# Shared-expert weights loaded at the head of the last attention body, its products spread over three chunks, the fourth part placed behind the body

## What is computed

```
x = x + tanh(g_xattn) * attention(layernorm(x), ctx_1024, ctxb_2048x32)
# attention: softmax(Q K^T * gate / sqrt(32)) V, then @ Wo + bo
xn = layernorm(x)
gs, us = xn @ wg_s, xn @ wu_s
out = (silu(gs) * us) @ wd_s                 # shared expert
out = out + sum over the top 2 of 16 experts of weight * ((silu(g) * u) @ wd_r)
x = x + tanh(g_ffn) * out
```

## Time and profile before

| what | value |
|---|---|
| median of 3 runs | 2016.85 us (2014.12 to 2017.68) |
| profiled execution, its own time | 2012.53 us |
| its span | 2010.8 us |
| PE busy | 1920.7 us (96%) |
| DVE / ACT / POOL busy | 1110.7 / 784.5 / 1225.4 us |
| DMA | 331.82 MB, mean 165 GB/s |
| last attention body | about 1376.4 to 1463.8 us |
| what stands behind it, up to the experts' phase | 1463.8 to 1499.1 us |

### The profile page before, as it was taken

One profiled execution on the slowest core, in us unless ns is written; L12 is line 12 of the kernel. 1 busy time (PEld: TensorE's weight loads), 2 busy tenths in 40 slices (PEclk: granted clock), 3 DMA queues, 4 the chain that ended last, 5 costly groups with the idle time before them and its releaser, 6 DMA issues. The chain is left out here.

```text
span 2010.8 us, 40479 instructions
## 1 busy us (share of the span) xinstructions
PE 1920.7 (96%) x12469; PEld 1494.6 (74%) x12470; DVE 1110.7 (55%) x1765; ACT 784.5 (39%) x1557; POOL 1225.4 (61%) x1383
## 2 busy tenths in 40 slices
PE   6799999999999999999999999999879999999799
PEld 5587877878787787878778787786658766666587
DVE  4556565656556566565656656565447533333287
ACT  3244454444545444454444445454432122222000
POOL 2377677776867777677777767675522533332463
PEclk9899999999999999999999999999889999999899
DMA  6754848466483755738375483746135454444787
GB/s 220 199 142 126 228 108 221 120 172 179 127 240 97 197 149 144 209 114 234 104 188 153 134 242 97 214 126 198 50 129 199 144 170 146 146 146 131 199 246 212
DMA packets 171275, 331.82 MB, mean 165 GB/s; under 512 B 20295, under 2 KB 69447, under 8 KB 170583
## 3 DMA queue, kind: packets, MB, share of 16 engines
q1 hardware_dynamic: 154316, 285.79, 49.9%
q0 software_dynamic: 10800, 33.30, 6.1%
q10 hardware_dynamic: 6112, 12.13, 1.8%
HBM read 214.83 MB, written 115.80 MB: 164 GB/s over the span
## 5 line engine op out<-in xcount | busy, mean ns | idle before, releaser
L940 DVE TENSOR_REDUCE neg_max<-score 112x1 f32<-112x750 f32 x512 | 480.7, 939 | 553.6 <-PE score L1246 552.1
L646 ACT ACTIVATE probs_t<-st 125x448 f32<-125x448 f32 x768 | 413.8, 541 | 501.9 <-PE st L1272 499.0
L515 POOL TENSOR_TENSOR acc<-acc,probs_t 125x448 f32<-125x448 f32 x256 | 310.4, 1212 | 53.9 <-ACT probs_t L646 52.7
L1272 PE MATMUL st<-q_stack,k_stack 98*125 98x224 f32 x1536 | 330.4, 297 | 3.1 <-DMA q_stack<-shift_rows 1.8
L1210 PE MATMUL proj<-ctx_hi,weights 128*128 128x376 f32 (+1 forms) x1024 | 329.2, 347 | 0.0
L517 POOL TENSOR_TENSOR acc<-acc,probs_t 125x448 f32<-125x448 f32 x256 | 295.0, 1152 | 20.1
L1272 PEld LDWEIGHTS st<-q_stack,k_stack 98*125 98x125 f32 x1536 | 266.4, 189 | 54.7 <-issue 24.9
L1246 PE MATMUL score<-k_stack,q_stack 96*112 96x512 f32 (+1 forms) x1024 | 283.5, 358 | 16.9 <-DMA k_stack<-k_parts 8.7
L1220 PE MATMUL proj<-weights,ctx_hi 128*125 128x512 f32 x768 | 248.8, 405 | 5.0 <-issue 5.0
L507 POOL TENSOR_TENSOR acc<-probs_t 125x448 f32<-125x448 f32 x128 | 145.7, 1140 | 163.8 <-PE pv L1323 145.5
L1246 PEld LDWEIGHTS score<-k_stack,q_stack 96*112 96x112 f32 x1024 | 160.1, 178 | 70.3 <-issue 46.7
(11 more groups left out here) (238 smaller groups left out, 2759.5 us busy)
## 6 DMA issues: line engine op xcount, KB each, us to landing
k_stack<-k_parts SPq DMA_DIRECT2D x192, 375.0 KB, 6.3
ctx_raw<-in_ctx_t SPq DMA_DIRECT2D x64, 375.0 KB, 9.9
k_parts<-k_hi SPq DMA_DIRECT2D x64, 375.0 KB, 6.8
k_parts<-k_lo SPq DMA_DIRECT2D x64, 375.0 KB, 7.4
y_slots<-y_sb SPq DMA_DIRECT2D x71, 256.0 KB, 3.0
q_stack<-q_parts SPq DMA_DIRECT2D x64, 224.0 KB, 6.0
gu_sb<-in_w_gu ACTq DMA_DIRECT2D x4, 2048.0 KB, 15.1
x_in<-in_x SPq DMA_DIRECT2D x16, 448.0 KB, 9.2
```

Of the source, the lines that this page charges most:

```text
L515: nc.gpsimd.tensor_tensor(both, both, tiles(c, p, pair, 0), ALU.add).then_inc(half_added, 1)
L646: act.activation(probs_t[0:KW, (c * PHASES + p) % 2, u % HC, :], st[u % 2][0:KW, 0:2 * L], ACT.Exp)\
L940: nc.vector.tensor_reduce(neg_max[:, h // HC % 2, h % HC, t:t + 1], score[0:QW, 0:S], axis=AX.X, op=ALU.max, negate=True).then_inc(maxed, 1)
L1272: ins = nc.tensor.matmul(st[u % 2][0:KW, k * L:(k + 1) * L], k_stack[0:SHIFTED, h, kt * KW:(kt + 1) * KW], q_stack[0:SHIFTED, h, :], start ...
```

## The change

The weights `gu_raw` are loaded at the head of the last body, right behind `load_stack(b, 3)`, without waiting for V5. For that they are placed elsewhere: three quarters in `gu_raw`, beginning where the context parts end, and the fourth in `gu_last`, in the place of the finished query weights. Two DMAs replace one. ACT makes the four high parts in ticks 8 to 11 of chunk 0 (before: ticks 1 to 4 of chunk 1), and splits the columns in ticks 6 and 7. DVE makes the low parts around the two pieces of head 11 (before: behind `normalize_output(b, 0)`). PE's product steps begin in tick 2 of chunk 1 and end with U2 in chunk 3: chunk 1 holds 12 triples (G0, U0, G1; before: 6), chunk 2 holds 8 (U1, G2; before: 12), chunk 3 holds 4 (U2; before: 14). G3 and U3, 8 triples, stand behind the body, after the output projection. The counts before are read off the places of `product` in the code. With G3 and U3 the last hidden part, the split of the next columns on ACT and DVE, and the order of the banks move.

```diff
-LAST = ("V4", "V5", "O0", "SH1", "O1", "G0", "SH2", "U0", "G1", "U1", "SH3", "G2", "YT0", "YT1", "LG", "U2", "G3", "U3")
+LAST = ("V4", "V5", "O0", "SH1", "O1", "G0", "U0", "SH2", "G1", "U1", "G2", "SH3", "YT0", "YT1", "LG", "U2")
+BEHIND = ("O0", "O1", "G3", "U3", "YT0", "YT1", "LG")
...
+            gu_last = last_use.enter_context(nc.sbuf_tensor("gu_last", [P, 2 * MID_S], F32))
...
-            last_use.enter_context(nc.sbuf_tensor("columns_end", [P, 3 * DC * GTOK], F32))
-            gu_raw = last_use.enter_context(nc.sbuf_tensor("gu_raw", [P, DC, 2 * MID_S], F32))
+            last_use.enter_context(nc.sbuf_tensor("context_end", [P, 2 * DC * S], F32))
+            gu_raw = last_use.enter_context(nc.sbuf_tensor("gu_raw", [P, DC - 1, 2 * MID_S], F32))
...
-                    sp.wait_ge(proj_done[bank_of(b, "V5")], turn_of(b, "V5") + 1)
-                    sp.dma_start(gu_raw[:, :, :], ws_gu).then_inc(shared_in, 16)
+                    sp.dma_start(gu_raw[:, :, :], ws_gu[:, 0:DC - 1, :]).then_inc(shared_in, 16)
+                    sp.dma_start(gu_last[:, :], ws_gu[:, DC - 1, :]).then_inc(shared_in, 16)
```

ACT in the body:

```diff
-                    if last and u in (6, 7, 9, 10):
-                        columns_high(0, (6, 7, 9, 10).index(u))
+                    if last and u in (6, 7):
+                        for d in (2 * u - 12, 2 * u - 11):
+                            columns_high(0, d)
+                    if last and u >= 8:
+                        shared_high(u - 8)
                     if u == 8:
                         place_shift(b, 1, b)
```

ACT behind the body:

```diff
+            for j in range(SC - 1):
+                silu(j)
+            for j in range(SC - 1):
+                hidden_high(j)
+            copy_product("G3", 3, gate_sb)
             copy_product("U3", 3, up_sb)
...
+            silu(SC - 1)
             act.wait_ge(x1_stored, B * 16)
             for t in range(QT):
                 normalize(x_res, t, xn2_ready, 2 * B - 1)
+            hidden_high(SC - 1)
             act.wait_ge(cols_stored, PRE["cols_stored"] + (B - 1) * 16)
             for t in range(QT):
                 copy_turned(B, f"YT{t}", t)
+            for d in range(DC):
+                columns_high(1, d)
```

DVE in the body:

```diff
                     result_statistics(b, 2 * b if last else 2 * b + 1, base)
+                if last:
+                    shared_low(0)
+                    shared_low(1)
                 next_maximum(b, 11, 0)
+                if last:
+                    shared_low(2)
+                    shared_low(3)
                 next_maximum(b, 11, 1)
                 normalize_output(b, 0, base, None if first else b)
```

DVE behind the body:

```diff
-            for j in range(1, SC):
+            for j in range(1, SC - 1):
                 hidden(j)
                 hidden_low(j)
             for t in range(QT):
                 add_result(B, t, B - 1)
             result_statistics(B, 2 * B - 1, base)
+            hidden(SC - 1)
+            hidden_low(SC - 1)
             for d in range(DC):
                 columns_low(1, d)
```

PE in chunk 1 (chunks 2 and 3 are changed in the same manner):

```diff
                 score_columns(b, 1, 2)
+                if last:
+                    product("G0", (0, 1))
...
                 score_columns(b, 1, 3)
+                if last:
+                    product("G0", (1, 2))
                 attend(b, 0, 2)
                 sum_up(b, 0)
                 next_scores(b, 11, 0)
...
                 score_columns(b, 1, 4)
+                if last:
+                    product("G0", (2, 3))
...
                 score_columns(b, 1, 5)
+                if last:
+                    product("G0", (3, 4))
...
                 score_columns(b, 1, 6)
+                if last:
+                    product("U0", (0, 2))
```

PE behind the body:

```diff
             down(0)
             for t in range(QT):
                 project_out(B - 1, t, B, (0, 4))
+            product("G3", (0, 4))
+            product("U3", (0, 4))
             for j in (1, 2):
                 down(j)
```

More of the change, by code:

```diff
@@ L1460, in batch @@
                 score_columns(b, 1, 7)
+                if last:
+                    product("U0", (2, 4))
                 attend(b, 1, 0)
-                if last:
-                    product("G0", (1, 2))
                 if not last:
@@ L1513, in batch @@
                 score_columns(b, 2, 3)
+                if last:
+                    product("U1", (3, 4))
                 attend(b, 1, 2)
@@ L1516, in batch @@
                 next_scores(b, 15, 0)
-                if last:
-                    product("G1", (1, 2))
                 if not last:
@@ L1549, in batch @@
                 score_columns(b, 2, 8)
-                if last:
-                    product("U1", (2, 3))
                 if not last:
@@ L1558, in batch @@
                 next_scores(b, 17, 0)
-                if last:
-                    product("U1", (3, 4))
                 if not last:
@@ L1564, in batch @@
                 attend(b, 2, 1)
-                if last:
-                    product("G2", (0, 1))
                 if not last:
@@ L1570, in batch @@
                 score_columns(b, 2, 11)
-                if last:
-                    product("G2", (1, 2))
                 if not last:
@@ L1579, in batch @@
                 next_scores(b, 18, 0)
-                if last:
-                    product("G2", (2, 3))
                 if not last:
@@ L1586, in batch @@
                 score_columns(b, 3, 1)
-                if last:
-                    product("G2", (3, 4))
                 next_scores(b, 18, 1)
@@ L1601, in batch @@
                     route(1, b)
-                if last:
-                    product("U2", (0, 2))
                 if not last:
@@ L1637, in batch @@
                 next_scores(b, 21, 0)
-                if last:
-                    product("U3", (0, 1))
                 if not last:
@@ L1643, in batch @@
                 attend(b, 3, 1)
-                if last:
-                    product("U3", (1, 2))
                 if not last:
@@ L1649, in batch @@
                 score_columns(b, 3, 11)
-                if last:
-                    product("U3", (2, 4))
                 if not last:
```

121 lines of the change are left out of this document (56 added, 65 removed).

## The result

The changed kernel ran at a median of 2022.83 us (2014.22 to 2029.3, 20 runs) beside 2015.93 us (2012.24 to 2025.87, 20 runs) for the kernel before on the same chip: ratio 1.0029, 95% interval [1.0019, 1.0039]. It is slower by 0.3%, about 6 us. The forecast was 1.9 us faster, and the range ended at 2020. The profiled execution took 2018.63 us (span 2016.9).

A forecast was written before the change was run, and what follows sets the result against it. Three stretches were taken to decide: chunk 1 (DVE and the clock), chunks 2 and 3 (PE, then POOL), the tail (one long chain). -1.4 - 2.5 + 2.0 = -1.9 us gave 2014.9 us, range 2010 to 2020.

The forecast's parts named there:

- Chunk 0: First chunk of the last body: ACT takes over four high parts, at no cost; length 21.1 us.
- Chunk 1: Second chunk: PE waits of 4.1 and 2.2 us, 3.8 us lost to the low clock; ends 1.4 us earlier.
- X: Start of chunk 2, 1429.1 us before; forecast at 1427.7, 1.4 us earlier.
- Chunks 2 and 3: Last two chunks: fewer products on PE, then POOL sets the pace; -2.5 us together, bounds -3.7 and 0.
- S: Start of the last `sum_up`, 1466.64 us before; forecast to move by -3.9 us.
- The tail: Behind the body: G3 and U3 partly fill PE's wait, DVE's totals end later; +2.0 us, bounds +0.5 and +3.5.
- The sum: Whole forecast up to the experts' block: -1.4 - 2.5 + 2.0 = -1.9 us.
- The clock did not stay low: Slower rival in chunk 1: the low clock holds, 10.3 us lost instead of 3.8, sum +4.6 us; chance 0.12.
- the loads were in time: Slower rival in chunk 0: two loads land after 1392, each microsecond late costing one; chance 0.03.
- it only moves work: Rival: POOL's end of chunk 3 comes no earlier (0 instead of -2.5), tail costs 2: 2017.4 us; chance 0.12.
- The rows named in the forecast as proof: Signs: chunk 1 waits of 4 and 2 us, clock above 0.7, `sum_up(3)` waiting 5 us, no wait before `turn_result`.

The follow-up runs named there:

- e2: The changed kernel, unchanged, timed and profiled again: ratio 1.0022 to the kernel before.
- e14: The changed kernel, unchanged, timed and profiled a third time: ratio 1.0031 to the kernel before.
- e5: The changed kernel with DVE's four totals and the copy of the logits put ahead of the four `columns_low`: ratio 0.9993 to the kernel before.
- e3: The changed kernel with G3 and U3 back in chunk 3 and the old ACT and DVE order behind the body: ratio 1.0003 to the kernel before.
- e7: The changed kernel with G3 and U3 back in chunk 3, `columns_high` and `columns_low` behind totals and logits copy: ratio 0.9978 to the kernel before.
- e8: The changed kernel with G3, U3 back in chunk 3, column splits behind the logits copy, `down(3)` ahead of `turn_result`: ratio 0.9994 to the kernel before.
- e10: The changed kernel with 32 idle matmuls at the start of TensorE's stream: ratio 1.0013 to the kernel before.
- e15: The changed kernel with DVE's totals and logits copy ahead of `columns_low`, plus 32 idle matmuls at TensorE's start: ratio 0.9982 to the kernel before.
- e6: The kernel before with only G3 and U3 moved behind the body, with the changed ACT and DVE order there: ratio 1.0028 to the kernel before.

## Why the prediction failed

**Chunk 0: right.** 21.1 us, as before.

**Chunk 1: right.** The waits were 3.77 and 2.04 us (forecast 4.1 and 2.2), the clock fell and came back (0.68, then 0.82), and X lay 51.52 us behind the start of chunk 0 instead of 52.73: -1.2 us (forecast -1.4). In the twelve profiles with this chunk X lay at 48.9 to 51.9, in the eight with the old one at 51.9 to 53.7, so chance moves it by up to 3 us, and one pair does not prove a gain of 1.2. The means do: 51.0 against 52.7, a gain of 1.7 us, with ranges that only touch.

**Chunks 2 and 3: right in kind, 1.2 us off in size.** Chunk 3 starts at X + 16.4 (forecast 17.2), with a wait of 0.57 us for POOL at `sum_up(2)`. From there POOL took 15.8 us instead of 16.4, where I had taken off 1.2. Two of its additions took 1.39 and 1.50 us instead of 1.13, at the time when DVE works on the hidden parts (1459.21 to 1461.45) (timeline of POOL, chunk 3, changed kernel):

```profile
1458.37 1.13 POOL L526 TENSOR_TENSOR acc<-acc,probs_t 125x448 f32<-125x448 f32 x1
1459.58 1.39 POOL L528 TENSOR_TENSOR acc<-acc,probs_t 125x448 f32<-125x448 f32 x1
1460.94 1.50 POOL L526 TENSOR_TENSOR acc<-acc,probs_t 125x448 f32<-125x448 f32 x1
```

S moved by -2.5 us, not -3.9; over three profiles of each kernel it is -2.9.

**The tail: 0.9 us too cheap.** I had the mechanism: DVE's totals stand behind `columns_low` and end 7.0 us behind `turn_result`, as forecast. The copy of the logits starts 6.9 us behind `turn_result` (1486.74 to 1493.64). `turn_result` came at S + 23.04 (forecast 23.6; 22.9 and 22.8 in e2 and e14). Missing from the sum was what follows that copy: from it to the load's issue it is 5.4 us instead of 3.7. Six stores stand on SP within 3.3 us (before: within 4.0), and the logits store lands 3.9 us after its issue instead of 2.9; that the closer stores make it late is not shown. From S to the load's issue it is 35.3 us instead of 32.4: +2.9, where the sum said +2.0. Together with S the block started 0.4 us later, counted from chunk 0, not 1.9 earlier; the means of B over three profiles of each kernel are equal, 122.7. Also missed was how much hangs on that order on DVE: e5 shows 3.1 to 3.5 us for it at the block's start, more than I had for the whole tail.

**Behind the block boundary: the failing step.** The sum ended at the boundary and carried everything behind it over at nothing, without a reason. There a 2.0 us longer T stood in the first profile of the changed kernel, 0.6 in the second and 6.5 in the third, 3.0 on average; 2.8 of the 6.5 are PE's low clock after its long wait for ACT. With B unchanged on average, that is 3.0 of the 4.4 to 6.2 us that the three timed comparisons show; the remainder is inside what their intervals leave open (2 to 4 us either way) and was found in no stretch. The forecast was a gain of 1.9 us: of the 6.3 to 8.1 us between it and the timed loss, this term is 3.0 and the block's start (0.0 on average instead of -1.9) is 1.9, as far as the profiles show it. What the later start of the vector work comes from in the change is partly open: taking G3 and U3 back moves the fetch from 2.3 us behind the issue to 7.8 ahead of it (e3), with the same number of TensorE's matmuls and weight loads, and `down(3)` ahead of `turn_result` moves it the other way (e7 to e8), again with the same number. Why an order of the work moves the fetch by 44 to 60 of them, I can't say.

**The rivals.** None described this. The clock did not stay low, the loads were in time, and "it only moves work" had POOL's end in chunk 3 unmoved, where chunks 2 and 3 gave 1.3 us of the 2.5, and put the result inside the band. The rows named in the forecast as proof were nearly all there, and the time was wrong: they all stood ahead of the boundary. POOL's power took 2.62 us beside DVE's `columns_low` (e3) and 0.70 without it (e7 and the changed kernel). The Trainium skill, GPSIMD Engine Reference, section 1, says that GpSimd contends with VectorE instructions that have two SBUF inputs; the traces agree, and the rule bears on more than I used it for.

**Open.** The order on DVE is worth 0.34% of the time between the changed kernel and e5 (the means of three and of one comparison), some 7 us, and 0.31% between e10 and e15, while the block's start shows 2.1 to 3.5 us. The landing differs from execution to execution of one kernel (5.4, 4.0, 7.0), and e5's profiled execution took 2004.05 us against its median of 1994.52, so its 9.1 us need not be typical; e8's took 1986.54 us against a median of 1995.11 in spite of its 6.4 us.

## What to carry to other kernels

A cut that shortens a body is worth what arrives at the next block's first loads: follow the last link over the boundary, the stores' landing and the order of the small operations on the engine that closes the phase, before counting what the body gains. Work that nobody needs soon (the split of the next columns) belongs behind the last operation that the boundary waits for; that alone turned the loss into par (e5). Where a small load stands at the head of a critical chain, look in its window for an instruction packet, since an edit of the instruction order alone can move one there (e3, e8). And take more than one profile of each kernel: here the first pair showed 4.2 us in a stretch that the second pair did not have.

## What the hardware showed

In five profiles a 16 KB instruction packet (0.95 to 1.66 us) began 1.1 to 2.0 us behind the issue of a 224 KB load, and the load landed after 4.7 to 9.1 us; with no instruction packet within 7 us, it landed after 3.3 to 4.2 us. Of three fetches at 2.2 to 2.35 us one went with a long landing (5.4). Late packets of 2 KB came 0.7 us apart in e5 and e6, beside another queue's 16 KB packets of 0.61 us. After waits of 3.3 to 6.1 us behind the block's start PE's granted clock fell to the lower level, and twelve matmuls took 4.2 to 4.9 us instead of 2.7. TensorE's instruction packets stood 260 matmuls and weight loads apart on average, singly 168 to 408. A padding of 128 moved the one near the load by 125 to 197 against the issue, one of 40 by 81, so that a packet's place is not the padding's sum. An fp32 matmul of 16 columns shows as two, of 0.19 us each at TensorE's start, so 32 of them filled 12.13 us.
